# One kernel, four edits: a shorter join, slots kept between stages, VectorE's convolution of one chunk, and row statistics in the last norm

## The reference

```python
h = _layernorm(x) * (1 + ca) + sa
x = x + ga * _L0_attn_ref(h, ...)      # attention, 8 heads of 8
h = _layernorm(x) * (1 + cb) + sb
x = x + gb * _L0_ffn_ref(h, ...)       # 8 experts, one per token by argmax
h = _layernorm(x) * (1 + ca) + sa      # second layer's own ca, sa, ...
x = x + ga * _L1_attn_ref(h, ...)      # state space
h = _layernorm(x) * (1 + cb) + sb
x = x + gb * _L1_ffn_ref(h, ...)       # per-head MLP on permuted features
```

```python
u, gate = jnp.split(hidden @ W_in.T, 2)
u = silu(causal_conv(u, conv_w, 4 taps) + conv_b)
dt, Bm, Cm = jnp.split(u @ Wx.T, [R, R + N])          # each then rms-normed
delta = softplus(dt @ Wdt.T + dt_bias)
state = exp(delta * A) * state + (delta * u) * Bm      # over 2048 time steps
y = (sum(state * Cm) + u * D_param) * silu(gate)
return y @ W_out.T
```

## Time and profile before

| what | us |
|---|---|
| median of 3 runs (lowest, highest) | 1741.63 (1739.49, 1743.62) |
| the profiled execution, and its span | 1740.03, 1738.1 |
| attention ends, experts' block starts | 499.9 |
| experts' block ends, state space starts | 710.2 |
| first scan, last output of the state space | 777.6, 1637.2 |
| last block begins, first gelu | 1640.4, 1692.4 |
| landing of the four transfers issued at 710 to 720: second half of `win` / `wout` / `convw` / `dpar`, from issue | 8.8 / 10.8 / 6.4 / 7.5 |
| landing of the eight stores of the normed chunks, from issue (min, median, max) | 5.3, 6.6, 8.7 |

### The profile page before, as it was taken

One profiled execution on the slowest core, in us unless ns is written; L12 is line 12 of the kernel. 1 busy time (PEld: TensorE's weight loads), 2 busy tenths in 40 slices (PEclk: granted clock), 3 DMA queues, 4 the chain that ended last, 5 costly groups with the idle time before them and its releaser, 6 DMA issues. The chain is left out here.

```text
span 1738.1 us, 26359 instructions
## 1 busy us (share of the span) xinstructions
PE 1458.2 (84%) x8976; PEld 795.6 (46%) x8976; DVE 1307.1 (75%) x2088; ACT 1134.2 (65%) x2288; POOL 923.5 (53%) x602
## 2 busy tenths in 40 slices
PE   5888999999975995788788898888999989847668
PEld 2441222222224442566366575665666656514332
DVE  3339999999318315117999999999999999999542
ACT  3323777777834333358787978879788787865238
POOL 0000000001000214427999999999999999999603
PEclk9875999999986996789799899998999999958789
DMA  6411112222037346733454554545455455544302
GB/s 252 163 40 43 31 29 77 80 81 74 3 77 271 114 127 241 261 86 80 113 143 98 135 134 109 140 118 128 116 135 135 109 123 123 133 104 119 113 36 97
DMA packets 156713, 199.34 MB, mean 115 GB/s; under 512 B 19823, under 2 KB 127255, under 8 KB 155043
## 3 DMA queue, kind: packets, MB, share of 16 engines
q1 hardware_dynamic: 142499, 163.93, 35.0%
q0 software_dynamic: 5168, 18.63, 3.3%
q10 hardware_dynamic: 8912, 15.09, 2.4%
HBM read 151.20 MB, written 46.34 MB: 114 GB/s over the span
## 5 line engine op out<-in xcount | busy, mean ns | idle before, releaser
L2084 DVE TENSOR_TENSOR_SCAN shared<-ssm_psum,ssm_state,shared 128x256 f32<-128x256 f32 x1024 | 674.8, 722 | 20.2 <-ACT ssm_state L1968 12.2
L1981 ACT ACTIVATE ssm_psum<-shared,ssm_a 128x256 f32<-128x256 f32 x1024 | 443.5, 468 | 152.2 <-DVE shared L2084 149.5
L1676 POOL TENSOR_TENSOR shared<-shared,ssm_bc 128x1024 f32<-128x1024 f32 x256 | 509.3, 2000 | 33.0 <-DVE shared L2084 15.8
L734 ACT ACTIVATE att_probs<-att_psum 128x1024 f32<-128x1024 f32 x256 | 248.4, 1021 | 76.6 <-PE att_psum L661 73.6
L1653 POOL TENSOR_TENSOR shared<-shared,ssm_bc 128x1024 f32<-128x1024 f32 x144 | 287.8, 1999 | 9.2 <-DMA shared<-drive_rows 9.2
L775 DVE TENSOR_REDUCE att_rowmax<-att_psum 128x1 f32<-128x512 f32 x448 | 277.7, 682 | 4.6 <-PE att_psum L634 2.9
L1801 PE MATMUL ssm_psum<-shared,ssm_select 128*32 128x256 f32 x2048 | 166.5, 415 | 81.5 <-POOL shared L1676 80.9
L603 POOL COPY att_v<-v_tokens 128x128 f32<-128x128 f32 x8 | 2.3, 292 | 298.8 <-ACT att_out L728 298.8
L634 PE MATMUL att_psum<-att_k,att_q 32*128 32x512 bf16 x448 | 138.5, 398 | 11.1 <-DVE att_rowmax L775 8.2
L673 PE MATMUL att_psum<-att_probs,att_v 128*32 128x512 f32 x1024 | 137.2, 608 | 0.6 <-ACT att_probs L734 0.6
L661 PE MATMUL att_psum<-att_q,att_k 32*128 32x512 bf16 (+2 forms) x1344 | 136.9, 385 | 0.0
(11 more groups left out here) (261 smaller groups left out, 1780.6 us busy)
## 6 DMA issues: line engine op xcount, KB each, us to landing
shared<-drive_rows SPq DMA_DIRECT2D x256, 256.0 KB, 4.4
qkv_wmod<-in_wmod SPq DMA_DIRECT2D x8, 1536.0 KB, 12.2
shared<-in_x SPq DMA_DIRECT2D x8, 1024.0 KB, 5.1
late_weights<-in_we SPq DMA_DIRECT2D x8, 1024.0 KB, 14.4
ssm_bc<-bc_rows SPq DMA_DIRECT2D x32, 256.0 KB, 5.2
drive_rows<-ssm_delta SPq DMA_DIRECT2D x64, 128.0 KB, 1.7
drive_rows<-ssm_du SPq DMA_DIRECT2D x64, 128.0 KB, 1.8
sorted_results<-moe_y ACTq DMA_DIRECT2D x23, 256.0 KB, 2.0
```

Source lines behind the costliest of these rows:

```text
L734: nc.scalar.activation(probs[:, u % RING, :].rearrange("p (j t) -> p j t", j=2), ps_s[u % 2], ACT.Exp).then_inc(exp_done, 1)
L1676: nc.gpsimd.tensor_tensor(read(Q), drive(Q), bc[:, c % 2, 1, gr, :].unsqueeze(1).to_broadcast([P, J, SW]), ALU.mult).then_inc(read_done, 1)
L1981: nc.scalar.activation(ps_decay[n % HALF_BANKS][:, i], rep[:, s % 2, 0, j, :], ACT.Exp, scale=amat[:, t, gr, j:j + 1]).then_inc(decay_done, 1)
L2084: nc.vector.tensor_tensor_scan(drive(Q)[:, j, :], ps_decay[(2 * Q + j // 2) % HALF_BANKS][:, j % 2], drive(Q)[:, j, :], state[:, t, gr, j: ...
```

## The change

**Experts' start.** The sums are loaded and stored as 128 rows of 128 numbers. `xw_in` is split in two semaphores: TensorE's first tiles wait for the first of the four transfers, tile 4 for the other three.

**Experts' end.** Chunk 0 has a slot of its own in `hnt` (`HN_SLOT`), is neither stored nor loaded again, and is modulated from that slot. The other seven share three slots. The wait for the stores of the sum moves from the block's end to the first load of the residual (`load_residual(0)`), far into the state space.

**State space's start.** VectorE convolves chunk 0: 2 tensor_scalar and 6 scalar_tensor_tensor instructions of 128x256 for each of four pairs. TensorE's `FIRST` has no `conv` of chunk 0; both gate pairs stand ahead of `rows`. ScalarE modulates chunk 1 and copies both gate pairs before silu. SyncE issues the small weights first.

**Last norm.** Mean and variance come out as 32 equal rows per quarter of the tokens. ScalarE copies the mean rows (L2268) and TensorE spreads them by four products with a row of ones. The variance is summed in two pairs, ScalarE computes exp(-0.5 ln(v + eps)) in rows, and four more products spread it. The turn, VectorE's inverse and the 16 small products are gone.

```diff
+HN_SLOT = (TSLOTS - 1,) + tuple(c % (TSLOTS - 1) for c in range(T // SW - 1))
...
-                sp.dma_start(hdst[:, :, i * SW:(i + 1) * SW], hnt[:, i % TSLOTS]).then_inc(g.hn_stored[i % TSLOTS], 16)
-            sp.wait_ge(x2_stored, 16 * SCH)
+                if i >= 1:
+                    sp.wait_ge(hn_out, (i + 1) * TC)
+                    sp.dma_start(hdst[:, :, i * SW:(i + 1) * SW], hnt[:, HN_SLOT[i]]).then_inc(g.hn_stored[HN_SLOT[i]], 16)
...
-            pe.wait_ge(xw_in, 16 * NCH)
...
+                if n == 0:
+                    pe.wait_ge(xw_in[0], 16)
+                if n == PER:
+                    pe.wait_ge(xw_in[1], 16 * (NCH - 1))
...
-            act.dma_start(sums[:], scratch.den.rearrange("h (p b) -> p h b", p=P)).then_inc(sums_in, 16)
+            act.dma_start(sums[:], scratch.den.rearrange("h (b t) -> (h b) t", t=HEADS * T // P)).then_inc(sums_in, 16)
...
-        FIRST = (("proj", 0, 0), ("proj", 0, 1), ("conv", 0, 0), ("proj", 0, 2), ("conv", 0, 1), ("proj", 0, 3), ("conv", 0, 2), ("conv", 0, 3),
-                 ("rows", 0, 0), ("square", 0, 0), ("rms", 0, 0), ("step", 0, 0), ("gate", 0, 0), ("gate", 0, 1), ("step", 0, 1))
+        FIRST = (("proj", 0, 0), ("proj", 0, 1), ("proj", 0, 2), ("proj", 0, 3), ("gate", 0, 0), ("gate", 0, 1),
+                 ("rows", 0, 0), ("square", 0, 0), ("rms", 0, 0), ("step", 0, 0), ("step", 0, 1))
...
-            sp.wait_ge(g.hn_stored[0], 16 * SCH // TSLOTS)
-            load_x(0)
...
+            for s in range(TSLOTS - 1):
+                sp.wait_ge(g.hn_stored[s], 16 * HN_SLOT[1:].count(s))
             load_x(1)
...
             copy_u(0, 1)
-            act.wait_ge(weights_in, 16 * 8)
-            copy_conv(0, 0)
             copy_u(0, 2)
-            copy_conv(0, 1)
             copy_u(0, 3)
-            copy_conv(0, 2)
-            copy_conv(0, 3)
+            modulate(1)
+            copy_gate(0, 0)
+            copy_gate(0, 1)
+            act.wait_ge(weights_in, 16 * 7)
+            act.wait_ge(g.hn_stored[2], 16 * HN_SLOT[1:].count(2))
             silu_u(0)
-            modulate(1)
...
+            def convolve(pair):
+
+                dve.wait_ge(upre_out, pair + 1)
+                for k in range(TAPS):
+                    for i in range(2):
+                        t = 2 * pair + i
+                        if k == 0:
+                            last = nc.vector.tensor_scalar(u[:, 0, t, :], upre[:, pair % 2, i, 0:SW], convw[:, t, 0:1], convb[:, t:t + 1], ALU.mult, ALU.add)
+                        else:
+                            dve.wait_ge(tap_done, (pair * (TAPS - 1) + k - 1) * 2 + i + 1)
+                            last = nc.vector.scalar_tensor_tensor(u[:, 0, t, :], upre[:, pair % 2, i, k:k + SW], convw[:, t, k:k + 1], u[:, 0, t, :],
+                                                                  ALU.mult, ALU.add)
+                        last.then_inc(conv_out if k == TAPS - 1 else tap_done, 1)
...
+                    last = nc.tensor.matmul(ps_stat[32 * i:32 * (i + 1), :], g.inv_d[:, 0:32], x[:, k, i * W:(i + 1) * W], start=(k == 0), stop=(k == KT - 1))
...
+                return nc.tensor.matmul(ps_wide[i], ones[32 * i:32 * i + 1, :], rows[32 * i:32 * i + 1, :], start=True, stop=True)
...
+            for pair in range(PAIRS):
+                pe.wait_ge(square_done, 2 * pair + 2)
+                for k in range(KT):
+                    for i in (2 * pair, 2 * pair + 1):
+                        last = nc.tensor.matmul(ps_var[pair][32 * i:32 * (i + 1), :], g.inv_d[:, 0:32], square[:, i, k, :], start=(k == 0), stop=(k == KT - 1))
+                last.then_inc(stat_mm, 1)
...
+                nc.scalar.activation(rstd_rows[r, :], ps_var[pair][r, :], ACT.Ln, bias=g.ln_eps[r, 0:1]).then_inc(rstd_step, 1)
+                act.wait_ge(rstd_step, 2 * pair + 1)
+                nc.scalar.activation(rstd_rows[r, :], rstd_rows[r, :], ACT.Exp, scale=-0.5).then_inc(rstd_step, 1)
```

120 lines of the change are left out of this document (76 added, 44 removed).

## The result

The changed kernel takes 1715.26 us (median of 4 runs, 1714.88 to 1716.98), the kernel before 1741.85 beside it (4 runs, 1739.49 to 1743.62): ratio 0.985, 95% interval 0.9833 to 0.9867. The forecast was 1725, so the gain is 26.6 us and not 16.6. The profiled execution took 1714.9 (span 1712.6, against 1740.0 and 1738.1 before), so the traces can be compared directly: the last store is issued at 1707.66, before at 1733.16, 25.5 sooner.

The account below looks back on a forecast made before the run. VectorE's scan stretch (778 to 1633 us) stays; only the road to it and what follows can move. Join 3.4, state-space start 3.3 and norm 9.4 give 16.1 off 1740.0, 1723.9; forecast 1725 us, range 1715 to 1733.

Parts of the forecast that it names:

- The likeliest case: Whole kernel: the forecast of 1725 us, with VectorE partly held by GpSimd in the convolution; chance 0.44.
- Rival 1: Chunk 0's convolution: GpSimd does not hold VectorE, silu follows the gate copies, 8.8 us more gained: 1716.5; chance 0.22.
- the holding: Chunk 0's convolution: VectorE operations wait for GpSimd's, ending at 743, losing 8.8 of a possible 12.1 us.
- the row: Earlier profile's one held VectorE operation: 1.23 us for 32 columns, ending 0.04 us after GpSimd's 1.26 us operation.
- The sum that ended at 740.2: Convolution's end if the fixed parts of both VectorE's and GpSimd's operations overlap: 4.8 us less than 745.0.
- The rule of the Trainium skill: Convolution: two-input VectorE and SBUF-reading GpSimd operations exclude each other for a whole instruction; end at 748.8.
- Boundary: Experts' end to first projection: SyncE's 3.9 us wait goes and chunk 0 needs no load; 5.1 us sooner.
- The list of signs: Closing list of trace signs that would show the forecast, such as first projection 4.9 us after the block starts.
- Join: Experts' start: sums land sooner and TensorE waits for one logits transfer, starting at 513.7 instead of 517.1; 3.4 us.
- Norm: Last norm: mean 2.5 us sooner, subtraction to first head product 6.9 us shorter; 9.4 us, between 6 and 11.
- Rival 3: Last norm: TensorE stays at half clock between short groups, variance pairs, spreads and first products included; 1730, chance 0.09.
- `rows` to the first scan: State space's start: everything from `rows` to the first scan stays as before, 27.9 us.

Follow-up runs that it names:

- The kernel with the boundary's wait: Changed kernel with SyncE again waiting for the eight stores of the sum at the experts' end: 1725.69 us, ratio 0.9913.
- the guard: Changed kernel with SyncE's wait back, and GpSimd's output-weight multiplications waiting for VectorE's convolution: 1722.53 us, ratio 0.99.
- the last kernel above: Changed kernel with silu ahead of the second gate copy, gelu's table loaded earlier, GpSimd's output-weight multiplications after the convolution: 1711.53 us, ratio 0.9832.

## Why the prediction was right, and where it wasn't

**Direction and mechanisms.** Faster by far more than 0.2%, as said with 0.94. The likeliest case was not the one that came. Rival 1 (0.22) came nearest, with its 1716.5 (1725 less its 8.8 is 1716.2) and its order, silu behind the gate copies; its mechanism, no holding at all, did not, for VectorE's operations took 0.52 us and not 0.42. The measured 1715.26 is in the range by a fraction of a us, and 2.4 us of the gain lie in stretches that no edit touches (below), so how near the edge it came is chance.

**The step that failed: the holding.** "I take 743, near the row": 8.8 of 12.1 us lost. Measured, VectorE's end costs nothing. Counted from the first projection, which itself came early, I had silu free at 32.4 us (743 less 710.6) and the trace has it at 22.5 (727.66 less 705.13), while the gate copies end at 24.1. The price of a turn was not what failed. The sum that ended at 740.2 has 0.50 us for a turn with a small operation (0.30 + 0.35 less 0.15) and 1.39 with a large one (0.30 + 1.24 less 0.15); measured are 0.52, and 1.4 with large ones of the same form. My own count at the measured prices, 24 x 0.52 + 8 x 1.4, gives 23.7 us and 740.8. I took 743, 2 us above that, for the row; that was the small part of the error.

What failed is which operations meet. I had GpSimd through 16 of its 40 small ones when VectorE begins, and so put the eight large ones, 9.9 us, into the convolution. In the trace GpSimd has begun four, VectorE's 32 operations meet only small ones and take 15.4 us (712.28 to 727.66). Even from my 717.1 that would end at 732.5, inside the gate copies' 734.3. The lead was wrong because I placed the two starts by different clocks: the projection from the old start of the block, without the join's gain, at 710.6, and the taps at 711.5, 5.2 us after my start of the block. The taps came at 711.2, which looks right, but that is 9.9 us after the block's start (701.31), and the projection came at 705.13. The kernel with the boundary's wait is the case that I forecast, with 21 small ones begun and the large ones met: there VectorE ends 29.8 us after the first projection, against 22.5 in the changed kernel, and `rows` comes 5.8 us later. With the guard, which takes the meeting away and nothing else, the 5.8 are gone but for 0.4.

The rule of the Trainium skill that I weighed ("SBUF — State Buffer", section "SBUF: two separate sides"), exclusion for a whole instruction, would have put the end at 748.8. The traces agree that one waits for the other, and not that it does so for the whole instruction: a turn lasts 0.52 us where the two alone are 0.41 and 0.35, 0.76 together, and 1.40 where they are 0.41 and 1.24, 1.65 together. The measurement decides: 0.24 to 0.25 us less than the sum in both. That these are the fixed parts, which overlap, fits and is not shown by itself.

**Boundary.** Forecast 5.1 from the experts' end to the projection, measured 6.2 (4.55 + 1.69): the wait went whole and took 0.6 more with it. Right. (The list of signs has 4.9 from the block's start to the projection; its own terms, 710.6 less 706.3, give 4.3, and the trace has 3.8.)

**Join.** Forecast 3.4, measured 2.1 in the trace. The mechanism of the layout was right, and the copy of the logits left ScalarE at 508.8, 9.7 us after the experts' start instead of 11.6; but I let the first transfer land in 3.5 us from its issue, a quarter of the group's 2.78 plus the last one's 2.8, and it took 5.33. The last of a group is no measure for the first.

**Norm.** Forecast 9.4, measured 9.7 by the last store (5.10 + 6.76 less 2.12). The sum is right by two errors that cancel: the mean's part gained 5.1 instead of 2.5, because the second half was there 14.9 us after the block's start instead of 15.4, its products took 1.92 us and not 3.4, and the spread 1.14 and not 1.7 (I had priced both at half clock); and "from the first product to the first gelu and on nothing changes" was wrong, with 0.85 for the exposed table load and the slower head products, and 1.3 after that. Rival 3 (variance at half clock) came true only in part: 8.72 us for all 32 records, at a granted clock of 0.52 until 1656 and of 1.00 from there.

**`rows` to the first scan.** "As before, 27.9": it took 29.35 and 28.01 in two profiles. TensorE idled 3.99 us before `rows` in both, and 4.24 before; the 16 products took 6.09 and 5.33, and 5.33 before. Up to GpSimd's first `ssm_du` the changed kernel is 0.6 us behind (16.0 us after `rows`, before 15.4); the other 0.85 lie in the way of the rows through device memory, 11.3 us from there to GpSimd's first product with them, before 10.4. The granted clock from 730 to 740 was 0.66, and 0.97 in the last kernel above:

```profile
730.00:740.00 10.00, 6.57 (x20) 3.70 (x20) 0.00 (x0) 4.38 (x5) 9.07 (x8) 0.66 0.00 0
```
```profile
730.00:740.00 10.00, 6.27 (x29) 3.94 (x29) 0.47 (x1) 4.77 (x9) 10.00 (x13) 0.97 0.01 3
```

(Columns as in the earlier trace rows; the changed kernel, then the last one.)

**The sum.** Join 2.1, state-space start 11.2 (4.55 + 1.69 + 6.48 less 1.49) against 3.3 forecast, norm 9.7 against 9.4: 23.1. The other 2.4 are in stretches that no edit touches: the first stage 0.8, the experts' tiles 1.4, the scans 0.2. The 1.4 are TensorE's clock at the first of the experts' products (8 records): 4.7 to 5.0 us in ten traces, at a granted clock of 0.73 to 0.79, and 6.2 to 6.3 in four, at 0.50. Before is one of the four, the changed kernel's first profile one of the ten and its second one of the four, so this is not the edits' doing.

```profile
567.54 6.25 PE L1104 MATMUL moe_psum<-late_weights,moe_ht 128*128 x8 [0.37 <-issue]
```
```profile
564.66 4.80 PE L1109 MATMUL moe_psum<-late_weights,moe_ht 128*128 x8 [0.21 <-ACT moe_ht L1171]
```

(Before; then the changed kernel.)

## What to carry to other kernels

Where two engines share a port, price the turn by the shape that meets it, and ask first which operations will meet at all: whether a transfer landed 1.2 us before the first projection or 6.1 us behind it decided here whether VectorE's longest operation took 0.6 or 10.4 us. Place both sides of such a meeting by the same start. An order that holds only by 1.6 us deserves a wait that makes it sure; the two kernels that have it show no cost (`rows` after 27.90 and 24.69 us), though it was not tried alone. Before calling a stretch the edit's, look at TensorE's granted clock in it: it made 1.4 us in the experts and 1.9 in the scans of kernels that don't differ there. Look for table loads behind the last wait, and put them beside it.

## What the runs showed of the hardware

- VectorE and GpSimd take turns, one instruction each, also for VectorE's one-input operations: 0.52 us a turn beside 128-column operations, 0.83 beside one-input and 1.16 to 1.4 beside two-input ones of 512 columns, where VectorE alone takes 0.41. Where both alone are known, the turn is 0.24 to 0.25 us shorter than their sum. In one execution a VectorE operation lasted 10.4 us, through eight GpSimd operations in a row; under what condition is open.
- The scans' stretch has two lengths, 862.7 to 863.1 and 865.2 to 866.2 us, in traces of different kernels on different chips. In the long ones (and in before) TensorE's granted clock falls to 0.5 for some 3 us at two places, and VectorE waits 0.85 or 0.89 us for it there; after the same pause of 1.28 us it did not fall in others. What decides it is open.
- The same 16 products took 3.64 us after a pause of 1.23 us and 6.09 after one of 3.99 (the clock granted in the 10 us around them 0.97 and 0.66). In the thirteen traces with pauses of 3.99 us or more they took 4.96 to 6.30.
